# GpSimd's sums of the down weights: around the first reduction of the roots, or behind both

## The chip, the core and the metric

The kernel runs on one core of a Trainium2 chip. The metric is the time of one execution on the device in microseconds. TensorE is called PE here, VectorE DVE, ScalarE ACT, GpSimd POOL, and SyncE, which issues nearly all DMAs, SP.

## What is computed

A gated feed-forward layer with a condition and quantised activations, then an adapter. x is 2 x 2048 tokens of 512 values; the hidden width is 2048, the adapter's 128.

```python
scale = cond @ norm_w.T + 1.0
h = x * (scale[:, None, :] * rsqrt(mean(x * x, -1) + 1e-6))
val, gate = split(h @ up_w.T, 2)
h = val * gelu(gate)
hq = act_quant(h)              # per token: 127 / max|h|, rounded
wq = weight_quant(down_w)      # one scale for all: -1, 0 or 1
x = hq @ wq.T + x
# adapter, its weights made from cond: Wd + (cond @ Wdd.T + bdd) / 10, Wu alike
out = x + relu(x @ Wd_b.T + bd) @ Wu_b.T + bu
```

## The kernel before

The 4096 tokens are 8 blocks of 512 (0 to 7), handled as 4 super-blocks `s` of two blocks each. For each super-block a loop runs over 16 chunks `j` of the hidden width; iteration `n = 16 s + j` is called a quad. In a quad, PE computes the up projection of one chunk for both blocks with seven products instead of eight (Strassen's scheme in the form with sums of tiles). One product is six matmuls of 512 columns. Its order in quad n is: product 1 and 5 of n, product 3 of n-1, product 6 of n, product 4 of n-1, product 2 and 7 of n, then "side work". Product 4 of n-1 waits for `val2(n-1)` on DVE (L1886), and product 7 of n for `seed_c(n)` on DVE (L1878).

DVE's instructions of one quad stand in a fixed order: the rows of the down projection of the quad before (`first_rows`, L1993 and L1995), `quantise` (L1976), `assemble` (L2112 and L2113, in quads 28, 29, 43 and 45), `multiply2` of n-1 (L1917, waits for ACT's gelu of product 3), `seed_c` (L1878), `multiply1` (L1927), the two running maxima (L1941), then in quad 27 `x_scaled(4)` (four times L1839) and `spread_roots(5)` (L1822), in quad 28 `x_scaled(5)`, and then `val2(n)` (L1886). The tensors named `_ps` lie in PSUM, all others in SBUF.

Down projection: super-block 0 is done plainly as side work of quads 26 to 29 (L1426). Super-blocks 1 and 2 use seven products of half width, which need four sums of quarters of the quantised down weights `wq`. GpSimd makes these four sums once, in super-block 1: `down_sums(3)`, `(1)`, `(0)` and `(2)`, each one `tensor_tensor` of 128 x 2048 fp8 values (L941), into `w_sums`, which lies over buffers 2 and 3 of the ring `w_ring`. SP writes them to DRAM once (`put_sums_down`, L676 to L678), and later loads them back before they are used. The load of ring buffers 2 and 3 for adapter weights of quad 30 (`load_w(82)` and `(83)`, L615) waits until this put has landed.

The norm of super-block s+1 is prepared in super-block s. For blocks 4 and up, GpSimd does it in two steps by reductions over the partitions: `square_total(i)` (L919), and `root_rows(i)` (L926). `root_rows(4)` waits for DVE's `spread_roots(4)`, which is issued in quad 26; `x_scaled(4)` on DVE waits for it in quad 27; then comes `spread_roots(5)`, `root_rows(5)`, and `x_scaled(5)` in quad 28. GpSimd also reduces the running maxima once for each super-block (`all_h`, L908).

GpSimd's order in super-block 1 is: `all_h(0)`, `square_total(4)`, `square_total(5)`, `down_sums` 3, 1, 0, `root_rows(4)`, `down_sums(2)`, `root_rows(5)`. SP's order in quad 29 is: two puts of rows, `put_sums_down`, `load_e(31)`, `load_l(30)` (the split up weights; they wait for PE's product 6 and 4), two loads of rows; in quad 30: `load_w(80)` to `(83)`, two puts of rows.

Of the kernel before, what the change touches and what calls it, by code (L numbers as in the profile page):

```python
# [135 lines left out]
def next_groups(n):  # L136

    return next(groups_of_quad(q) for q in range(n, NQ) if q in DW_QUADS)
# [105 lines left out]
def build(nc, x, cond, norm_w, up_w, down_w, Wd, bd, Wu, bu, Wdd, bdd, Wdu, bdu, out):  # L244
    aux = aux_plan()
    aux_keys = list(aux)
    with ExitStack() as ctx:
# [287 lines left out]
        def _(sp):  # L535
# [140 lines left out]
            def put_sums_down():  # L676
                sp.wait_ge(s_wsum, 4)
                sp.dma_start(ws_dram, w_sums).then_inc(s_wsum_dma, 16)  # L678
# [90 lines left out]
            for n in range(NQ):  # L769
                s, j = divmod(n, NP)  # L770


                if n > NP + 1:
                    for g in groups_of_quad(n):
                        load_w(2 * g)
                        load_w(2 * g + 1)
                if s == 1 and j in DOWN_QUANTISE:
                    load_d(8 + DOWN_QUANTISE.index(j))
                if n:
                    for g in groups_of_quad(n - 1):  # L780
                        move(g)
                if s == 0:
                    if 1 <= j and j + 4 < NP:
                        load_u(j + 4)
                    if j:
                        put_l(j)
                    if n == 1 or n - 1 in DW_QUADS:
                        for g in next_groups(n):
                            load_w(2 * g)
                            load_w(2 * g + 1)  # L790
                    if j == 4:
                        put_sums()
                    if 3 <= j < 11:
                        load_d(j - 3)
                    if 1 <= j and j + 1 < NP:
                        put_e(j + 1)
                if s == 1 and Y_FIRST < j <= Y_FIRST + 4:
                    put_row(2 * (j - Y_FIRST - 1))
                    put_row(2 * (j - Y_FIRST - 1) + 1)
                if s == 1 and j == 13:  # L800
                    put_sums_down()
                if s > 1 and j == 10:
                    load_c11(s - 1)
                if s > 0 and j == 10 and s < NSB - 1:
                    load_base(s - 1)
                if s > 1 and j == 10:
                    load_sums_down(s - 1)
                if s > 1 and j == 11:
                    put_c11(s - 1)
                if s > 1 and j == 13:  # L810
                    load_c22(s - 1)
                    load_c21(s - 1)
                if s > 1 and j == 14:
                    put_c21(s - 1)
                if NP <= n + 2 < NQ:
                    load_e(n + 2)
                if NP <= n + 1 < NQ:
                    load_l(n + 1)
                if j in NEXT_X:
                    load_x(s + 1, NEXT_X[j])  # L820
                if s == 1 and Y_FIRST <= j < Y_FIRST + 4:
                    load_row(2 * (j - Y_FIRST))
                    load_row(2 * (j - Y_FIRST) + 1)
                if s > 1 and j == 11:
                    load_c12(s - 1)
                if s > 1 and j == 14:
                    put_second(s - 1)
                if n == max(ASSEMBLE) + 1:
                    load_ad(0)
                    load_ad(1)  # L830
                for at, i in MID_AT.items():
                    if n == at + 3:
                        put_ad(i)
                        if i == 0:
                            load_ad(2)
                if n == NQ - 2:
                    load_ad(3)
# [24 lines left out]
        @block.gpsimd  # L862
        def _(pool):
            pool.memset(ones[:, :], 1.0).then_inc(s_const, 1)
            pool.memset(ident[:, :], 1.0).then_inc(s_const, 1)
            pool.wait_ge(s_const, 2)
            pool.affine_select(out=ident[:, :], in_=ident[:, :], compare_op=ALU.is_equal, fill=0.0,
                               base=0, pattern=[[-1, P]], channel_multiplier=1).then_inc(s_const, 1)

            def a_block(j, half, which):  # L870
                return u_raw(j)[:, 2 * half:2 * half + 2, P * which:P * which + P]

            def weight_sums(j):

                pool.wait_ge(s_u[j % 4], 16 * (j // 4 + 1))
                if j == 2:

                    aux_ready(pool, "dw", 2)
                elif j == 4:
                    aux_ready(pool, "dw", 3)  # L880
                elif j == 0:

                    pool.wait_ge(s_seed_c, 1)
                elif j >= 3:
                    if j == 6:
                        pool.wait_ge(s_sums_lo, 2)
                    pool.wait_ge(s_ulo, part_count(j - 2, 3))
                s1, s2, s3, s4 = (s_sum(j, n, n + 1).rearrange("p (k m) -> p k m", k=2)
                                  for n in range(4))
                pool.tensor_tensor(s1, a_block(j, 0, 0), a_block(j, 1, 0), ALU.add)\  # L890
                    .then_inc(s_us, 1)
                pool.wait_ge(s_us, sum_count(j, 1))
                pool.tensor_tensor(s2, s1, a_block(j, 0, 1), ALU.subtract).then_inc(s_us, 1)
                pool.tensor_tensor(s3, a_block(j, 0, 1), a_block(j, 0, 0), ALU.subtract)\
                    .then_inc(s_us, 1)
                pool.wait_ge(s_us, sum_count(j, 2))
                pool.tensor_tensor(s4, a_block(j, 1, 1), s2, ALU.subtract).then_inc(s_us, 1)

            def all_h(s):

                if s:
                    pool.wait_ge(s_x1, 2 * KD * s)
                for t, s_max in ((1, s_max2), (0, s_max1)):
                    pool.wait_ge(s_max, NP * (s + 1))
                    if s == NSB - 1 and t == 0:

                        pool.wait_ge(s_step, 1)
                    pool.partition_all_reduce(yscale[:, TB * t:TB * t + TB],  # L908
                                              hmax[:, TB * t:TB * t + TB], P, AR.absmax)\
                        .then_inc(s_ma[t], 1)  # L910


            pool.wait_ge(s_rs, 2)
            for j in SUM_ORDER:
                weight_sums(j)
            def square_total(i):

                pool.wait_ge(s_sqp, (KD - 1) * (i - 1))
                pool.partition_all_reduce(res[:, 3, :], res[:, 2, :], P, AR.add)\  # L919
                    .then_inc(s_square_total, 1)  # L920

            def root_rows(i):

                pool.wait_ge(s_root_grid, i - 3)
                pool.wait_ge(s_xs, KD * i)
                pool.partition_all_reduce(res[:, 2, :], res[:, 3, :], P, AR.add)\  # L926
                    .then_inc(s_root_rows, 1)

            a11, a21, a12, a22 = (wq[:, HC * half:HC * half + HC, 2 * P * low:2 * P * low + 2 * P]
                                  for half in range(2) for low in range(2))  # L930

            def down_sums(m, left, right, op):

                if m == 3:
                    pool.wait_ge(s_wq, 8)
                    aux_ready(pool, "dw", AFTER_DOWN // 2 - 1)
                elif m == 1:
                    pool.wait_ge(s_wsum, 1)
                elif m == 0:
                    pool.wait_ge(s_wsum, 2)  # L940
                pool.tensor_tensor(w_sums[:, m, :, :], left, right, op, saturate=False)\  # L941
                    .then_inc(s_wsum, 1)

            for s in range(1, NSB):
                all_h(s - 1)
                if s + 1 < NSB:
                    for t in range(2):
                        square_total(2 * s + 2 + t)
                    if s == 1:
                        down_sums(3, a21, a22, ALU.add)  # L950
                        down_sums(1, w_sums[:, 3, :, :], a11, ALU.subtract)
                        down_sums(0, a12, w_sums[:, 1, :, :], ALU.subtract)
                    root_rows(2 * s + 2)
                    if s == 1:
                        down_sums(2, a11, a21, ALU.subtract)
                    root_rows(2 * s + 3)
            all_h(NSB - 1)

        @block.scalar
# [1413 lines left out]
```

## Time and profile before

| | |
|---|---|
| median of 3 runs | 840.19 us (839.9 to 841.25) |
| the profiled execution's own time | 839.96 us |
| its span, first to last instruction | 838.2 us |
| PE busy | 823.3 us, 98% |
| DVE busy | 661.7 us, 79% |
| ACT busy | 397.4 us, 47% |
| POOL busy | 119.9 us, 14% |
| DMA engines busy, slices 293 to 314, 314 to 335, 335 to 356 us | 6, 2 and 3 tenths |
| granted TensorE clock | 1.00 of full speed over the span |

Times of the profile are microseconds from the first instruction. A row of a timeline has the start, the duration, the engine, the line of the kernel, the operation, its output and inputs with their shapes, and in brackets how long the engine had been idle before and what ended that; "issue" stands for idle time that ended on nothing the profile shows. Neighbouring instructions of one kind are merged into one row ("x2"). A matmul's record is longer than the time to the next one's start, since they overlap.

### The profile page before, as it was taken

Reading aid. Unit: us, or ns where it says so; the run is one execution under the profiler, and the core shown is the slowest. Engines: PE = TensorE matmul, PEld = TensorE weight load, DVE = VectorE, ACT = ScalarE, POOL = GpSimd, SP = SyncE. Lnnn points to the kernel's source line nnn. Section 1 sums busy time; section 2 is a strip of 40 time slices with the busy share of each in tenths; the row PEclk is TensorE's granted clock in tenths of the full one; section 3 lists DMA queues with packets and bytes.
Section 4 is the critical chain, followed back from the end, with each engine's and each line's share of the span. In section 5 each row is a group of like instructions: output and inputs, shape, how many; then the busy total and the mean of one; then the engine's idle time right before and its main releaser. Section 6 shows DMA issues by size and latency. Waiting matters only on the chain.

```text
span 838.2 us, 11811 instructions
## 1 busy us (share of the span) xinstructions
PE 823.3 (98%) x3902; PEld 358.0 (43%) x3902; DVE 661.7 (79%) x964; ACT 397.4 (47%) x649; POOL 119.9 (14%) x91
## 2 busy tenths in 40 slices
PE   6999999999999999999999999999999999999998
PEld 4334444444444434444444444444444444444443
DVE  5997887989878889767777678988975666675986
ACT  5778887766455532227445543326433333324000
POOL 0363332302001053200101011100200000001000
PEclk9999999999999999999999999999999999999999
DMA  9879988666999862378798866337247444435232
GB/s 345 337 263 346 341 292 297 234 219 221 307 346 372 322 215 107 138 258 281 277 327 306 299 222 190 115 93 259 86 127 232 138 129 155 137 95 176 101 126 75
DMA packets 64859, 186.64 MB, mean 223 GB/s; under 512 B 7072, under 2 KB 8352, under 8 KB 64416
## 3 DMA queue, kind: packets, MB, share of 16 engines
q1 hardware_dynamic: 64512, 185.63, 63.9%
q8 instruction: 32, 0.52, 0.3%
q10 hardware_dynamic: 288, 0.26, 0.1%
q14 instruction: 27, 0.22, 0.1%
HBM read 154.41 MB, written 30.41 MB: 220 GB/s over the span
## 4 chain that ended last, share of the span: by engine, by line
PE 90%; DVE 2%; issue 2%; DVEq 0%
PE b_ps L1326 9%; PE b_ps L1328 9%; PE b_ps L1330 9%; PE a_ps L1326 6%; PE aux_ps L1381 6%; PE a_ps L1328 6%; PE a_ps L1330 6%; PE aux_ps L1439 6%; PE aux_ps L1526 3%; PE aux_ps L1517 3%; PE c_ps L1326 3%; PE e_ps L1328 3%; PE e_ps L1326 3%; PE e_ps L1330 3%; PE c_ps L1328 3%; PE c_ps L1330 3%
## 5 line engine op out<-in xcount | busy, mean ns | idle before, releaser
L1917 DVE SCALAR_TENSOR_TENSOR h_ring<-v_sb,unscale,gelu 128x512 f32<-128x512 f32 x63 | 55.1, 874 | 67.5 <-issue 35.4
L1326 PE MATMUL b_ps<-t_mov,u_l 128*128 128x512 f16 x252 | 95.5, 379 | 2.7 <-DVE c_ps L1878 2.7
L1330 PE MATMUL b_ps<-t_mov,u_l 128*128 128x512 f16 x252 | 95.5, 379 | 0.0
L1328 PE MATMUL b_ps<-t_mov,u_l 128*128 128x512 f16 x252 | 95.5, 379 | 0.0
L1941 DVE TENSOR_TENSOR hmax<-gelu,hmax 128x512 f32<-128x512 f32 x120 | 88.6, 740 | 7.8 <-ACT gelu L1090 2.9
L1060 ACT ACTIVATE b_ps<-a_ps 128x512 f32<-128x512 f32 x63 | 36.7, 582 | 99.1 <-PE a_ps L1330 99.1
L1094 ACT ACTIVATE gelu<-h_ring 128x512 f32<-128x512 f32 x64 | 40.3, 630 | 65.8 <-DVE h_ring L1917 65.8
L1976 DVE TENSOR_TENSOR h_ring<-h_ring,qscale 128x1024 f16<-128x1024 f32 x48 | 64.7, 1388 | 0.0
L1076 ACT ACTIVATE gelu<-a_ps,unscale 128x512 f32<-128x512 f32 x64 | 43.7, 682 | 43.4 <-DVE hmax L1941 41.1
L908 POOL PARTITION_ALL_REDUCE yscale<-hmax x8 | 17.9, 2267 | 321.4 <-DVE hmax L1941 320.7
L1090 ACT ACTIVATE gelu<-h_ring 128x512 f32<-128x512 f32 x64 | 40.2, 628 | 45.6 <-DVE h_ring L1927 45.3
L1927 DVE SCALAR_TENSOR_TENSOR h_ring<-b_ps,unscale,gelu 128x512 f32<-128x512 f32 x64 | 47.8, 747 | 16.1 <-PE b_ps L1330 15.8
L1084 ACT ACTIVATE gelu<-c_ps,unscale 128x512 f32<-128x512 f32 x64 | 43.9, 686 | 32.9 <-PE c_ps L1330 32.9
L1381 PE MATMUL aux_ps<-w_ring,cond_sb 128*32 128x512 f32 x480 | 58.3, 599 | 0.0
L1067 ACT ACTIVATE p_sb<-e_ps 128x512 f32<-128x512 f32 x63 | 37.5, 595 | 37.3 <-PE e_ps L1330 27.6
L1886 DVE TENSOR_TENSOR v_sb<-b_ps,p_sb 128x512 f32<-128x512 f32 x63 | 43.2, 686 | 11.3 <-PE b_ps L1330 11.1
L1326 PE MATMUL b_ps<-t_mov,u_e 128*128 128x512 f16 x126 | 47.8, 379 | 0.9 <-DVE t_mov L1870 0.9
L1326 PE MATMUL e_ps<-t_mov,u_e 128*128 128x512 f16 x126 | 47.8, 379 | 0.2 <-DVE u_e L1706 0.2
L1326 PE MATMUL a_ps<-t_mov,u_e 128*128 128x512 f16 x126 | 47.9, 381 | 0.0
L1328 PE MATMUL e_ps<-t_mov,u_e 128*128 128x512 f16 x126 | 47.8, 379 | 0.0
L1330 PE MATMUL e_ps<-t_mov,u_e 128*128 128x512 f16 x126 | 47.8, 379 | 0.0
L1326 PE MATMUL a_ps<-t_mov,u_l 128*128 128x512 f16 x126 | 47.8, 379 | 0.0
(253 smaller groups left out, 1690.3 us busy)
## 6 DMA issues: line engine op xcount, KB each, us to landing
w_ring<-in_Wdu SPq DMA_DIRECT2D x64, 512.0 KB, 6.2
w_ring<-in_Wdd SPq DMA_DIRECT2D x56, 512.0 KB, 7.2
u_l<-ul_dram SPq DMA_DIRECT2D x48, 512.0 KB, 4.7
u_e<-ue_dram SPq DMA_DIRECT2D x48, 384.0 KB, 3.2
h_ring<-in_up_w SPq DMA_DIRECT2D x16, 512.0 KB, 6.5
x_sb<-in_x SPq DMA_DIRECT2D x8, 1024.0 KB, 8.2
res<-in_down_w SPq DMA_DIRECT2D x16, 512.0 KB, 7.4
ul_dram<-u_l SPq DMA_DIRECT2D x15, 512.0 KB, 5.7
```

The costliest lines, as they stand in the source:

```text
L1076: act.activation(gelu1[:, :], a_ps[n % 2][:, :], ACT.Gelu, scale=unscale[:, s // 2, j:j + 1]).then_inc(s_g1, 1)
L1084: act.activation(gelu2[:, :], c_ps[:, :], ACT.Gelu, scale=unscale[:, s // 2, j:j + 1]).then_inc(s_g2, 1)
L1326: pe.matmul(ps[:, :], weight(n, p, 0, k), hi, start=fresh and k == 0, stop=False, skip_group_check=True)
L1328: pe.matmul(ps[:, :], weight(n, p, 0, k), lo, start=False, stop=False, skip_group_check=True)
L1330: mm = pe.matmul(ps[:, :], weight(n, p, 1, k), hi, start=False, stop=k == 1, skip_group_check=True)
L1381: mm = pe.matmul(ps[32 * q:32 * q + 32, :], cond_sb[:, :], w_tile(n)[:, 512 * (q % 2):512 * (q % 2) + 512], start=True, stop=True)
L1439: mm = pe.matmul(ps[:, :], w, q_slot(d, at + c)[:, TB * t:TB * t + TB], start=fresh and c == 0, stop=c == HC - 1, skip_group_check=True)
L1886: dve.tensor_tensor(v_sb[:, :], b_ps[n % 2][:, :], p5_sb[:, :], ALU.add)\
L1917: dve.scalar_tensor_tensor(out=h_slot(n)[:, TB:TS], in0=val[:, :], scalar=unscale[:, s // 2, j:j + 1], in1=gelu2[:, :], op0=ALU.mult, op1= ...
L1927: dve.scalar_tensor_tensor(out=h_slot(n)[:, 0:TB], in0=b_ps[n % 2][:, :], scalar=unscale[:, s // 2, j:j + 1], in1=gelu1[:, :], op0=ALU.mul ...
L1941: dve.tensor_tensor(total, absolute, total, ALU.max).then_inc(done, 1)
L1976: dve.tensor_tensor(q_slot(s, c), h_slot(NP * s + c), qscale[:, :], ALU.mult)\
```

## The change

In GpSimd's program both `root_rows` of the super-block now come ahead of all four `down_sums`; before, three sums stood ahead of the first and one between the two. In super-block 2, which has no sums, the order is as it was. In SP's program `put_sums_down` moves within quad 29 from ahead of `load_e(31)` to behind the two loads of rows.

```diff
                 if s == 1 and Y_FIRST < j <= Y_FIRST + 4:
                     put_row(2 * (j - Y_FIRST - 1))
                     put_row(2 * (j - Y_FIRST - 1) + 1)
-                if s == 1 and j == 13:
-                    put_sums_down()
                 if s > 1 and j == 10:
                     load_c11(s - 1)
...
                 if s == 1 and Y_FIRST <= j < Y_FIRST + 4:
                     load_row(2 * (j - Y_FIRST))
                     load_row(2 * (j - Y_FIRST) + 1)
+                if s == 1 and j == 13:
+                    put_sums_down()
...
                 if s + 1 < NSB:
                     for t in range(2):
                         square_total(2 * s + 2 + t)
+                    for t in range(2):
+                        root_rows(2 * s + 2 + t)
                     if s == 1:
                         down_sums(3, a21, a22, ALU.add)
                         down_sums(1, w_sums[:, 3, :, :], a11, ALU.subtract)
                         down_sums(0, a12, w_sums[:, 1, :, :], ALU.subtract)
-                    root_rows(2 * s + 2)
-                    if s == 1:
                         down_sums(2, a11, a21, ALU.subtract)
-                    root_rows(2 * s + 3)
```

## Rows read from the trace of the kernel before

**Rows 1.** Waits of PE, 200 to 400 us: us in total, times, longest.

```profile
PE b_ps L1326 <- DVE c_ps L1878: 1.7, 2, 1.3
```

**Rows 2.** Timeline of GpSimd, 300 to 345 us: start, us, engine, line, idle before.

```profile
305.04 3.82 POOL L941 TENSOR_TENSOR w_ring<-wq 128x2048 fp8e4<-128x2048 fp8e4 x1 [9.62 <-issue]
308.94 4.17 POOL L941 TENSOR_TENSOR w_ring<-w_ring,wq 128x2048 fp8e4<-128x2048 fp8e4 x1
313.18 4.16 POOL L941 TENSOR_TENSOR w_ring<-wq,w_ring 128x2048 fp8e4<-128x2048 fp8e4 x1
323.12 3.25 POOL L926 PARTITION_ALL_REDUCE res<-res  x1 [5.79 <-issue]
334.29 3.82 POOL L941 TENSOR_TENSOR w_ring<-wq 128x2048 fp8e4<-128x2048 fp8e4 x1 [7.91 <-issue]
```

**Rows 3.** Timeline of DVE beside GpSimd's operations, 305 to 338 us.

```profile
305.78 3.63 DVE L1917 SCALAR_TENSOR_TENSOR h_ring<-v_sb,unscale,gelu 128x512 f32<-128x512 f32 x1 [1.89 <-issue]
...
310.59 3.05 DVE L1941 TENSOR_TENSOR hmax<-gelu,hmax 128x512 f32<-128x512 f32 x1
...
313.57 4.31 DVE L1941 TENSOR_TENSOR hmax<-gelu,hmax 128x512 f32<-128x512 f32 x1
...
323.76 2.15 DVE L1917 SCALAR_TENSOR_TENSOR h_ring<-v_sb,unscale,gelu 128x512 f32<-128x512 f32 x1
...
335.80 0.69 DVE L1995 TENSOR_TENSOR res<-aux_ps,res 128x512 f32<-128x512 f32 x1
336.40 2.25 DVE L2112 TENSOR_TENSOR l_wd<-l_wd,w_ring 128x512 f32<-128x512 f32 x1
```

**Rows 4.** Timelines of DVE and PE: the two product 7 that waited.

```profile
309.33 0.69 DVE L1878 TENSOR_TENSOR c_ps<-b_ps,p_sb 128x512 f32<-128x512 f32 x1
...
310.17 0.38 PE L1326 MATMUL b_ps<-t_mov,u_l 128*128 128x512 f16 x1 [1.32 <-DVE c_ps L1878]
...
326.66 0.38 PE L1326 MATMUL b_ps<-t_mov,u_l 128*128 128x512 f16 x1 [0.36 <-DVE c_ps L1878]
```

**Rows 5.** Timelines of DVE and PE in iterations 28 and 29.

```profile
342.21 1.47 DVE L1941 TENSOR_TENSOR hmax<-gelu,hmax 128x512 f32<-128x512 f32 x2
...
347.29 2.74 DVE L1839 SCALAR_TENSOR_TENSOR x_sb<-res,cs_x,x_sb 128x512 f32<-128x512 f32 x4 [3.61 <-POOL res L926]
...
349.94 0.68 DVE L1886 TENSOR_TENSOR v_sb<-b_ps,p_sb 128x512 f32<-128x512 f32 x1
...
355.70 0.75 DVE L1917 SCALAR_TENSOR_TENSOR h_ring<-v_sb,unscale,gelu 128x512 f32<-128x512 f32 x1 [1.09 <-ACT gelu L1084]
356.37 0.69 DVE L1878 TENSOR_TENSOR c_ps<-b_ps,p_sb 128x512 f32<-128x512 f32 x1
...
342.63 0.38 PE L1326 MATMUL b_ps<-t_mov,u_l 128*128 128x512 f16 x1
...
358.60 0.38 PE L1326 MATMUL b_ps<-t_mov,u_l 128*128 128x512 f16 x1
```

**Rows 6.** Timelines of DVE (both super-blocks) and GpSimd around spread_roots.

```profile
331.12 0.68 DVE L1822 TENSOR_TENSOR res<-ident,rs 128x512 f32<-128x512 f32 x1
...
514.52 0.69 DVE L1822 TENSOR_TENSOR res<-ident,rs 128x512 f32<-128x512 f32 x1
...
515.31 3.23 POOL L926 PARTITION_ALL_REDUCE res<-res  x1 [23.15 <-DVE res L1822]
```

**Rows 7.** Timelines of SP's queue and PE: put, weight loads, use.

```profile
353.70 0.43 SPq L678 DMA_DIRECT2D ws_dram<-w_ring  x1
...
358.88 3.05 SPq L615 DMA_DIRECT2D w_ring<-in_Wdu  x4
...
375.96 1.92 PE L1381 MATMUL aux_ps<-w_ring,cond_sb 128*32 128x512 f32 x16
```

**Rows 8.** Timeline of PE near the start: single and merged.

```profile
17.88 0.63 PE L1364 MATMUL a_ps<-t_mov,u_e 128*128 128x512 f16 x1
...
18.31 1.06 PE L1368 MATMUL a_ps<-t_mov,u_e 128*128 128x512 f16 x2
```
## The prediction

> **What bounds the kernel now.** I read the page's busy shares first: PE is busy 98% of the span, so a microsecond counts only if PE stands still for it or stops standing still. The waits of PE between 200 and 400 us come next: one kind is left there, product 7's first matmul waiting for DVE's `seed_c` (L1878), twice [rows 1]. The timeline of GpSimd shows why to look at DVE: the three sums of `down_sums` lie at 305.04 to 317.34, the fourth at 334.29, and the first `root_rows` reduction at 323.12 [rows 2]. Beside them DVE's operations with two SBUF inputs are stretched. L1917 takes 3.63 us and ends 0.55 us behind the first sum; the two L1941 take 3.05 and 4.31 us and end 0.53 and 0.54 us behind the second and the third; L1917 takes 2.15 us beside a reduction; L2112 takes 2.25 us beside the fourth sum [rows 3]. L1995, with one input in PSUM, takes its usual 0.69 us beside that same sum [rows 3]. So while GpSimd runs a sum, a DVE operation with two SBUF inputs waits until it ends. The two engines take turns too: the third sum began at 313.18, was let in between two L1941 that DVE had back to back, and the second of these waited for it. One turn costs 313.18 - 308.94 = 4.24 us; DVE, whose own operation would have taken 0.67 of it, loses 3.57.
>
> **What the change removes.** Both stalls of PE come from this. The first sum holds L1917 of iteration 26, so `seed_c` is late and PE stands 1.32 us before product 7; `root_rows(4)` holds L1917 of iteration 27 and costs 0.36 us [rows 4]. A matmul is recorded 0.38 us long and the next starts 0.22 us behind it, so each idle time hides 0.16 us more: 1.48 + 0.52 = 2.00 us. With the sums gone from there, `seed_c` of iteration 26 isn't held, DVE ends its list earlier, and `root_rows(4)` needs no change of GpSimd's code ahead of it (the reduction before it is of the same kind), so it runs earlier by what the three sums held DVE (2.9, 2.3 and 3.6 us over the usual times of these operations), near 314, beside no L1917. Both stalls go: -2.0 us. What is late next there is L1917 itself, which waits for ScalarE's gelu, and then has 1.4 us to spare before product 7 (in iteration 29 `seed_c` ends at 357.06, PE could start 0.15 behind, and product 7 starts at 358.60 [rows 5]). The wait of `x_scaled(5)` for `root_rows(5)`, 3.61 us [rows 5], goes too, but PE never felt it: worth nothing by itself.
>
> **Where the sums land.** `root_rows(5)` starts when `spread_roots(5)` ends; in the next super-block, where no sum is in the way, the reduction of `root_rows(6)` starts 0.1 us behind L1822 [rows 6]. DVE comes to `spread_roots(5)` (L1822) at 331.12 before [rows 6]. Its list then hangs on product 7 of iteration 27, which moves from 326.66 to 324.66, and by the pattern of iteration 28, where L1941 starts 0.42 us before product 7 (342.21 against 342.63 [rows 5]), x_scaled(4) and the spread follow by 328.96. The reduction runs 3.25 us: 329.1 to 332.3. Now GpSimd changes from the code of the reduction to that of the element-wise sum. The profile shows this as idle time on "issue": 9.62 and 7.91 us in this direction, 5.79 us in the other [rows 2]. By the page's slices the DMA engines were 6 tenths busy around the longest and 2 tenths around the other; where the changed kernel's falls they are 2 to 3 tenths busy, so 9.62 is the less likely of the two, and the code of the first sum may come sooner than either. I bound it by 5.8 and 7.9 us, with 9.6 as a tail, and take the middle, 6.9 us: **the first sum starts at 339.2** (338.1 to 340.2, tail 341.9). [...]
>
> **What it costs there.** In iteration 28, all 2.0 us earlier than before, DVE has ahead of it: two L1941 at 340.2 (1.47 us), four L1839 of `x_scaled(5)` (2.65 us for the four), `val2` L1886 (in PSUM), four operations of y rows (in PSUM), L2112, L2113, L1917, `seed_c` [rows 5]. The first six have two SBUF inputs. One passes per sum: the first sum ends at 343.0 and lets one L1941 end at 343.6; the second ends at 347.3, L1941 at 347.8; the third at 351.5, L1839 at 352.0; the fourth at 355.7, L1839 at 356.3. The two L1839 left take until 357.5, where `val2` starts. From the start of `val2` to the end of L2113 are 4.67 us (349.94 to 354.61, where the idle time ahead of L1917 begins), then L1917 0.67 and `seed_c` 0.69, and PE 0.15 behind (`seed_c` ended at 310.02, product 7 began at 310.17): 6.2 us [rows 4, 5]. Product 7 of iteration 29 can start at 363.7. Unheld it would start at 358.60 - 2.00 = 356.6 [rows 5]. Loss: 7.1 us, seen as two waits: product 4 of iteration 28 needs `val2` (358.2 + 0.15, against 354.0, twelve matmuls of 0.216 us ahead of product 7: some 4.4 us), and product 7 `seed_c` (some 2.7 us). The same from the other side: the first L1941 is held 2.7 us (340.9 to 343.6) and three operations 3.57 us each, 13.4 in all; DVE's slack in this stretch is 3.61 us of idle before L1839, 1.09 before L1917 and 1.4 before product 7, 6.1 in all: 7.3. **Sum: -2.0 + 7.1 = +5.1 us.** By the bounds of the code change it is +4.0 (start 338.1) to +6.1 (start 340.2).
>
> **The put.** In the diff `put_sums_down` moves behind load_e(31), load_l(30) and the two loads of rows in SP's iteration 29, so from 353.70 to just ahead of 358.88, 5.1 us later; load_w(82) and (83) wait for it and stand ahead of put_row(6), (7). The four weight loads were issued by 361.9 and first used at 375.96 [rows 7]: 14 us of cover, of which 5 go, and PE is 5 us later itself. GpSimd ends the sums at some 355.7, before SP comes to that wait. Nothing for the put. With its cover gone it would cost a microsecond for each late. What load_e(31) and load_l(30) gain by standing ahead is nothing either: they wait for PE's own products. After the sums GpSimd has nothing until the super-block's last maximum, three quads on, so a code change back is hidden.
>
> **Rivals.**
> - *The sums start later than L1941.* If the code takes 9.6 us again, both L1941 and one L1839 are through; three sums hold three L1839, `val2` is at 355.1, and the fourth runs beside the rows in PSUM and holds L2112 only to 359.3. Product 7 starts at 361.5: loss 4.9, net +3.0: 843.2 us. For it: both rows of this direction; against: the DMA load around the 9.6.
> - *The clock.* PE stands over 4 us in one piece. After the standstill at the start of the kernel two matmuls of 512 columns take 1.06 us together and one of them 0.63 [rows 8]: they start 0.43 apart, against 0.22 elsewhere: the 1.2 GHz level, though the granted clock reads 1.00. If that comes back here, product 4 and 2 (12 matmuls, 2.6 us more) hide under the second wait, product 7's six and up to twelve of the next rows don't: +1.3 to +3.9, 846.6 to 849.2, likeliest 847.9. Against: no stall above 1.5 us lies inside the kernel to judge by. [...]
> - *Faster.* The turns go to DVE: if GpSimd waits whenever DVE has the next operation of two SBUF inputs ready, the sums just stretch, nobody waits for them, and only the 2.0 us gain stays: 838.2 us. It decides where the sums hold no more than two of the nine such operations up to `seed_c` (7.2 us, against 6.1 of slack and 2.0 won). Against it: the third sum got in between two L1941.
> - *Nothing.* The first sum starts behind 344, past x_scaled: holds of 1.2, 3.6 and 3.6 us on L2112, L2113 and L1917, less 6.1, are 2.3 us against 2.0 won: 840.5.
>
> **How the numbers follow.** Forecast: 840.19 + 5.1 = 845.3 us (the profiled run was 839.96, with a span of 838.2; the median is 0.2 above it, so 845.1 for a run like it). Chances: the forecast's case (start 337 to 341.5) 0.60, later start 0.15, clock 0.10, nothing 0.05, faster 0.10. Range 841.6 to 848.6: it takes in the forecast's bounds (844.2 to 846.3), the later start, and most of the clock case, and leaves the last two out. Slower by over 0.2% (1.7 us, about what can be told from no change here) 0.85, within 0.05, faster 0.10.
>
> **What would show it.** In the profile after: no wait of PE for c_ps L1878 near 309 and 325; `root_rows(4)` near 313.7 and (5) near 329; the first sum near 339 and the four 4.2 us apart; L1941 and L1839 of 3 to 4 us beside them; two waits of PE of about 4.4 and 2.7 us near 354 and 361, on L1886 and L1878; SP's ws_dram issue behind the row loads with no long wait. Wrong if L1839 keeps its 0.75 us beside a sum, if the four sums are far more than 4.2 us apart, or if PE waits for w_ring near 377.

## The result, and the profile after

The changed kernel takes 845.36 us (median of 6 runs, 844.8 to 847.48) against 840.26 us of the kernel before (6 runs, 839.41 to 842.54): a ratio of 1.0064, with a 95% interval of 1.0052 to 1.0076. It is slower by 5.4 us by the ratio. The profiled execution took 846.51 us. Line numbers from 956 on are one lower than before (L1886 is L1885, L1878 is L1877, L1941 is L1940, L1839 is L1838, L1917 is L1916).

The page of the kernel after: span, busy shares of PE, and the granted clock in 40 slices.

```profile
span 844.8 us, 11807 instructions
...
PE 826.8 (98%) x3902; PEld 358.5 (42%) x3902; DVE 663.0 (78%) x964; ACT 397.6 (47%) x649; POOL 121.8 (14%) x91
...
PEclk9999999999999999989999999999999999999999
```

PE's busy share is as it was, but one slice shows a lower clock, and the share of 98% hides a stall of over 4 us. The waits of PE from 200 to 400 us show it. The two stalls of [rows 1] are gone, and another stands in their place: product 4 of quad 28 waits for `val2(28)`.

```profile
PE b_ps L1325 <- DVE v_sb L1885: 4.2, 1, 4.2
```

GpSimd's timeline (start, duration, engine, line, operation, idle before). Both reductions stand ahead of the sums; `root_rows(4)`, at 323.12 in [rows 2], is at 315.03, and the idle time between the last reduction and the first sum is 6.91 us, less than the 7.91 and 9.62 of [rows 2]. In GpSimd's queue two instructions `MODIFY_POOL_CONFIG`, issued for the sums' line L941, stand at 333.6, where the second reduction ends. In the kernel before such a pair stands ahead of each of the four idle times: for L941 at 295.4 and 326.4 (9.62 and 7.91 us), for L926 at 317.5 and 338.3 (5.79 and 5.90 us). In neither kernel does one stand between two sums, nor in the changed one ahead of `root_rows(4)` at 315.03, which follows another reduction. This is what "code change" means here; what GpSimd does in the idle time is not in the trace. The four sums start 3.9 to 4.2 us apart.

```profile
315.03 3.23 POOL L926 PARTITION_ALL_REDUCE res<-res  x1 [18.14 <-DVE res L1821]
330.42 3.23 POOL L926 PARTITION_ALL_REDUCE res<-res  x1 [12.16 <-DVE res L1821]
340.56 3.82 POOL L941 TENSOR_TENSOR w_ring<-wq 128x2048 fp8e4<-128x2048 fp8e4 x1 [6.91 <-issue]
344.46 4.16 POOL L941 TENSOR_TENSOR w_ring<-w_ring,wq 128x2048 fp8e4<-128x2048 fp8e4 x1
348.70 4.16 POOL L941 TENSOR_TENSOR w_ring<-wq,w_ring 128x2048 fp8e4<-128x2048 fp8e4 x1
352.82 4.27 POOL L941 TENSOR_TENSOR w_ring<-wq 128x2048 fp8e4<-128x2048 fp8e4 x1
```

DVE's timeline beside them. Each of the first four operations with two SBUF inputs waits for one sum, just as in [rows 3], and ends 0.55 us behind it: both running maxima (L1940) and two of the four L1838 of `x_scaled(5)`. The last two take their usual time, then come `val2(28)` (L1885) and, 5.2 us later, `seed_c(29)` (L1877).

```profile
341.58 3.35 DVE L1940 TENSOR_TENSOR hmax<-gelu,hmax 128x512 f32<-128x512 f32 x1
...
344.86 4.31 DVE L1940 TENSOR_TENSOR hmax<-gelu,hmax 128x512 f32<-128x512 f32 x1
349.09 4.32 DVE L1838 SCALAR_TENSOR_TENSOR x_sb<-res,cs_x,x_sb 128x512 f32<-128x512 f32 x1
...
353.33 4.31 DVE L1838 SCALAR_TENSOR_TENSOR x_sb<-res,cs_x,x_sb 128x512 f32<-128x512 f32 x1
...
358.89 0.68 DVE L1885 TENSOR_TENSOR v_sb<-b_ps,p_sb 128x512 f32<-128x512 f32 x1
...
364.13 0.69 DVE L1877 TENSOR_TENSOR c_ps<-b_ps,p_sb 128x512 f32<-128x512 f32 x1
```

PE's timeline: product 4 starts at 359.71, behind `val2(28)`, which ended at 359.57. From there to the second matmul of product 7 the records last some 0.6 us and the starts lie 0.43 us apart (360.09, 360.51, 360.94), not 0.22. Product 7 starts at 364.97, where [rows 5] had 358.60. It still goes by `seed_c(29)`, which ended at 364.82, 0.15 us before; no idle time stands between, since slow matmuls had filled the wait but for the last 0.2 us.

```profile
359.71 0.58 PE L1325 MATMUL b_ps<-t_mov,u_l 128*128 128x512 f16 x1 [4.16 <-DVE v_sb L1885]
360.09 0.63 PE L1327 MATMUL b_ps<-t_mov,u_l 128*128 128x512 f16 x1
...
364.36 0.63 PE L1329 MATMUL a_ps<-t_mov,u_l 128*128 128x512 f16 x1
364.97 0.58 PE L1325 MATMUL b_ps<-t_mov,u_l 128*128 128x512 f16 x1
...
366.47 7.07 PE L1425 MATMUL aux_ps<-h_ring,wq 128*128 128x512 f16 x32
```

The stretch from 350 to 372 us and the part of it from 360 to 364 us (length, busy times, granted clock, DMA share, GB/s): the granted clock is 0.84 over the whole and 0.50 over the part. It was 1.00 before.

```profile
350.00:372.00 22.00, 17.84 (x70) 7.14 (x69) 18.65 (x19) 3.70 (x6) 7.09 (x2) 0.84 0.44 149
360.00:364.00 4.00, 4.00 (x11) 1.39 (x10) 3.90 (x7) 0.83 (x2) 0.00 (x0) 0.50 0.42 145
```

The put was issued at 364.71, where [rows 7] had 353.70. The four weight loads behind it took 9.70 us to issue, because two of them wait for the put, and they are first used at 382.54. PE did not wait for them. (PE's one wait for `w_ring` in this trace, 0.18 us, lies at 268.22, far ahead of the change.)

```profile
364.71 0.43 SPq L678 DMA_DIRECT2D ws_dram<-w_ring  x1
365.24 9.70 SPq L615 DMA_DIRECT2D w_ring<-in_Wdu  x4
...
382.54 1.92 PE L1380 MATMUL aux_ps<-w_ring,cond_sb 128*32 128x512 f32 x16
```

The rows of y of quads 27 to 29 (the L1425 group of PE) measure the loss without the rest of the run. Undisturbed they are 15.97 us apart; here those of quads 28 and 29 start at 343.30 and 366.47, 23.17 apart: **7.2 us are lost in quad 29.** The execution as a whole is 1.4 us late by quad 26 from something else: in quad 22 PE and its weight loader waited for a late load of adapter weights. That is a matter of this one execution (`e5_after_again` is 0.4 us late there), and it is why the span grew by 6.6 us while the medians are 5.1 apart.

### The profile page after: what moved, and what is told of

Its sections match the earlier page's. It is cut to its first block, busy times and chain, and to the rows that moved or that the text cites. A ratio compares the mean times of both kernels' runs of the same rounds, so it can differ in the third digit from the quotient of the medians.

```text
span 844.8 us, 11807 instructions
## 1 busy us (share of the span) xinstructions
PE 826.8 (98%) x3902; PEld 358.5 (42%) x3902; DVE 663.0 (78%) x964; ACT 397.6 (47%) x649; POOL 121.8 (14%) x91
## 4 chain that ended last, share of the span: by engine, by line
PE 89%; DVE 2%; DMA 1%; issue 1%; SPq 0%; DVEq 0%
PE b_ps L1325 9%; PE b_ps L1329 9%; PE b_ps L1327 9%; PE a_ps L1325 6%; PE aux_ps L1380 6%; PE a_ps L1329 6%; PE a_ps L1327 6%; PE aux_ps L1438 6%; PE aux_ps L1525 3%; PE aux_ps L1516 3%; PE c_ps L1325 3%; PE c_ps L1327 3%; PE c_ps L1329 3%; PE e_ps L1325 3%; PE e_ps L1329 3%; PE e_ps L1327 3%
## 5 line engine op out<-in xcount | busy, mean ns | idle before, releaser
L1916 DVE SCALAR_TENSOR_TENSOR h_ring<-v_sb,unscale,gelu 128x512 f32<-128x512 f32 x63 | 50.9, 808 | 73.4 <-ACT gelu L1083 37.9
L1940 DVE TENSOR_TENSOR hmax<-gelu,hmax 128x512 f32<-128x512 f32 x120 | 89.0, 743 | 7.9 <-ACT gelu L1089 3.0
L908 POOL PARTITION_ALL_REDUCE yscale<-hmax x8 | 17.8, 2260 | 318.1 <-DVE hmax L1940 317.5
L1885 DVE TENSOR_TENSOR v_sb<-b_ps,p_sb 128x512 f32<-128x512 f32 x63 | 43.2, 686 | 11.2 <-PE b_ps L1329 11.0
L1325 PE MATMUL a_ps<-t_mov,u_l 128*128 128x512 f16 x126 | 48.3, 383 | 0.0
L1327 PE MATMUL a_ps<-t_mov,u_l 128*128 128x512 f16 x126 | 48.3, 383 | 0.0
L1329 PE MATMUL a_ps<-t_mov,u_l 128*128 128x512 f16 x126 | 48.3, 383 | 0.0
L1325 PE MATMUL e_ps<-t_mov,u_e 128*128 128x512 f16 x126 | 47.8, 379 | 0.5 <-DVE u_e L1705 0.5
```

The source lines that it names most:

```text
L1325: pe.matmul(ps[:, :], weight(n, p, 0, k), hi, start=fresh and k == 0, stop=False, skip_group_check=True)
L1327: pe.matmul(ps[:, :], weight(n, p, 0, k), lo, start=False, stop=False, skip_group_check=True)
L1329: mm = pe.matmul(ps[:, :], weight(n, p, 1, k), hi, start=False, stop=k == 1, skip_group_check=True)
L1885: dve.tensor_tensor(v_sb[:, :], b_ps[n % 2][:, :], p5_sb[:, :], ALU.add)\
L1916: dve.scalar_tensor_tensor(out=h_slot(n)[:, TB:TS], in0=val[:, :], scalar=unscale[:, s // 2, j:j + 1], in1=gelu2[:, :], op0=ALU.mult, op1= ...
L1940: dve.tensor_tensor(total, absolute, total, ALU.max).then_inc(done, 1)
```

## The experiments

The theory: GpSimd and DVE take turns by whole instructions, so every sum holds one DVE operation with two SBUF inputs, and the sums now stand where six such operations precede `val2(28)` and nine precede `seed_c(29)`. The rivals: the later put makes the loss; the reductions or the code change make it; GpSimd's busy time counts, whatever its pieces. Ratios are against runs of the kernel before on the same chip, each with its 95% interval.

### The two halves of the change

Only GpSimd's order (`e1_order_only`):

```diff
                     put_row(2 * (j - Y_FIRST - 1) + 1)
+                if s == 1 and j == 13:
+                    put_sums_down()
...
                     load_row(2 * (j - Y_FIRST) + 1)
-                if s == 1 and j == 13:
-                    put_sums_down()
```

> The changed kernel with put_sums_down in its old place, so only GpSimd's order is changed. Theory (the holds of DVE by the sums make all of the loss, the put makes none): 845.3 us, between 844.5 and 846; SP reaches the put behind the end of the sums and does not wait; the wait of 0.2 us of PE for w_ring may go. Rival (the later put makes a part of the loss, since the weight loads queue behind it): 840.5 to 844.

Measured: 845.91 us, ratio 1.0069 (1.0056 to 1.0082). Only the put, `e2_put_only`, is the same edit the other way round on the kernel before.

> The kernel before with only the put moved behind the two loads of rows; GpSimd's order is the old one. Theory: 840.2 us, no change that can be measured (839.5 to 841), both old stalls of PE before product 7 stay. Rival (the put costs): 842 or more.

Measured: 839.33 us, ratio 0.9999 (0.9990 to 1.0008), with both old stalls in place. So the whole loss is GpSimd's order; the put neither costs nor gains anything beyond the 0.8 us of that interval. It isn't unseen, though: in its new place it took 8.6 us to land (9.4 in the changed kernel), beside the loads issued just around it, where before it took 4.2. Two of the weight loads wait for it, but PE does not.

PE's timeline of `e1_order_only` holds one thing more. The clock stays up for the first two matmuls after the wait and falls from the third (359.44) on; it recovers at 362.85, before product 7, which therefore shows a wait of its own for `seed_c(29)`.

```profile
359.01 0.38 PE L1325 MATMUL b_ps<-t_mov,u_l 128*128 128x512 f16 x1 [3.93 <-DVE v_sb L1885]
...
359.87 0.63 PE L1325 MATMUL b_ps<-t_mov,u_l 128*128 128x512 f16 x1
...
364.27 0.38 PE L1325 MATMUL b_ps<-t_mov,u_l 128*128 128x512 f16 x1 [0.82 <-DVE c_ps L1877]
```

### The sums taken away (e3_small_sums) and two of them (e6_two_sums)

```diff
-                pool.tensor_tensor(w_sums[:, m, :, :], left, right, op, saturate=False)\
+                cut = (slice(0, 1), slice(0, 32)) if m in (0, 1, 2, 3) else (slice(0, HC), slice(0, 2 * P))
+                pool.tensor_tensor(w_sums[:, m, cut[0], cut[1]], left[:, cut[0], cut[1]],
+                                   right[:, cut[0], cut[1]], op, saturate=False)\
                     .then_inc(s_wsum, 1)
```

In `e6_two_sums` the condition is `m in (0, 2)`. The sums that run first, `down_sums(3)` and `(1)`, are then whole. Both kernels leave most of the cut sums unmade, and both put `wq` to DRAM in place of `w_sums`.

> The changed kernel with each of the four sums cut to 32 values of each partition, and the put taken from wq instead of w_sums, so the products of the down projection that use the sums are not those of the reference. All semaphores, waits, the code change of GpSimd and the size of the put are kept. Theory: no hold of DVE is left, the gain of the two old stalls stays alone: 840.2 - 2.0 = 838.2 us, no wait of PE for L1877 or L1885 between 300 and 370 us. Rival (the loss comes from the later reductions, the code change or the put): 843 to 845.

Measured: 838.54 us, ratio 0.9984 (0.9975 to 0.9993). GpSimd and DVE in it: the first sum still comes 7.09 us behind the reduction, the first small sum lasts 0.23 us, and the maxima and the four L1840 (`x_scaled(5)`) take their usual times. PE waits for nothing there.

```profile
339.88 0.23 POOL L942 TENSOR_TENSOR w_ring<-wq 128x32 fp8e4<-128x32 fp8e4 x1 [7.09 <-issue]
...
340.72 1.47 DVE L1942 TENSOR_TENSOR hmax<-gelu,hmax 128x512 f32<-128x512 f32 x2
342.11 2.73 DVE L1840 SCALAR_TENSOR_TENSOR x_sb<-res,cs_x,x_sb 128x512 f32<-128x512 f32 x4
```

> The changed kernel with the first two of the four sums at full size and the other two cut to 32 values a partition; the put comes from wq, so the products that use the sums are not those of the reference. Theory (one DVE operation is held for each full sum, first 2.7 then 3.57 us, against 6.1 us of slack): 6.3 - 6.1 = 0.2 us of wait, so 840.2 - 2.0 + 0.2 = 838.4 us, no wait of PE for L1885 near 355. Rival (each sum costs its share of the 7.1 us, two of them 3.5): 841.7 us.

Measured: 839.10 us, ratio 0.9983 (0.9973 to 0.9992). The first two sums hold both maxima (7.55 us instead of 1.47), and the loss ends there: `x_scaled(5)` is free, DVE works without a gap into L1918 (`multiply2`), and PE has no wait in this stretch. `seed_c(29)` ends at 356.39, 0.33 us before product 7 starts at 356.72, so the slack is nearly used up.

```profile
340.32 7.55 DVE L1942 TENSOR_TENSOR hmax<-gelu,hmax 128x512 f32<-128x512 f32 x2
347.80 2.73 DVE L1840 SCALAR_TENSOR_TENSOR x_sb<-res,cs_x,x_sb 128x512 f32<-128x512 f32 x4
...
355.04 0.74 DVE L1918 SCALAR_TENSOR_TENSOR h_ring<-v_sb,unscale,gelu 128x512 f32<-128x512 f32 x1
```

6.1 us of delay cost nothing, all four sums cost 7: what counts is the delay above DVE's slack, not a share for each sum. The rival that wanted 3.5 us for two sums falls, and the code change and the moved reductions, present here and in `e3_small_sums`, are cleared as well.

### The sums in pieces (e4_split_sums, e10_two_pieces, e11_split_again)

```diff
-                pool.tensor_tensor(w_sums[:, m, :, :], left, right, op, saturate=False)\
-                    .then_inc(s_wsum, 1)
+                for c in range(0, HC, HC // 8):
+                    part = slice(c, c + HC // 8)
+                    pool.tensor_tensor(w_sums[:, m, part, :], left[:, part, :],
+                                       right[:, part, :], op, saturate=False)\
+                        .then_inc(s_wsum, 1)
```

The three waits on `s_wsum` count eight times as far (twice in `e10_two_pieces`, where 8 is 2).

> The changed kernel with each sum issued as eight instructions of 256 values a partition instead of one of 2048; the same work. Theory (the two engines take turns by whole instructions): a DVE operation with two SBUF inputs waits for one piece at most, about 0.5 us; up to nine such operations lose 4.5 us at most, less than the slack of 6.1: no wait of PE, 838.2 us. Rival (GpSimd's busy time beside DVE counts, whatever its pieces): the sums take 16 to 18 us as before, DVE is held as long, 845 us.

Measured: 839.00 us, ratio 0.9985 (0.9976 to 0.9993). The same work now takes GpSimd 24 us instead of 16, and DVE loses 0.4 us on the maxima (1.86 instead of 1.47) and 1.5 on `x_scaled(5)` (4.26 instead of 2.73). The rival that counts GpSimd's busy time falls: there is more of it, and PE doesn't wait. The put now waits for the last piece and is issued at 364.09; the last weight load behind it is issued at 369.8, for a use that starts at 374.39, so its cover is down to 4.6 us.

```profile
339.67 7.51 POOL L943 TENSOR_TENSOR w_ring<-wq 128x256 fp8e4<-128x256 fp8e4 x8 [6.95 <-issue]
...
359.24 4.82 POOL L943 TENSOR_TENSOR w_ring<-wq 128x256 fp8e4<-128x256 fp8e4 x8
...
340.64 1.86 DVE L1943 TENSOR_TENSOR hmax<-gelu,hmax 128x512 f32<-128x512 f32 x2
342.42 4.26 DVE L1841 SCALAR_TENSOR_TENSOR x_sb<-res,cs_x,x_sb 128x512 f32<-128x512 f32 x4
```

> The changed kernel with each sum in eight pieces, once more, for a narrower interval against the kernel before and beside the other two: 838.9 us, a ratio of 0.9985.

Measured: 838.41 us, ratio 0.9988 (0.9979 to 0.9997). With its two intervals just below 1, this version beats both kernels, if by only 0.12 to 0.15% of the time of the kernel before.

> The changed kernel with each sum issued as two instructions of 1024 values a partition. Theory of turns: a held DVE operation waits for one piece, 1.9 us and a little, and loses 1.7 us; two L1940 and four L1838 lose 9.4 us before val2(28), less 6.1 us of slack: 3.3 us of the 7.1 are left: 840.2 - 2.0 + 3.3 = 841.5 us. Rival (GpSimd's busy time beside DVE counts): 845.5 us. Rival (any split cures it): 838.8 us.

Measured: 843.25 us, ratio 1.0042 (1.0029 to 1.0055), 3.5 us slower: between the two rivals, as the theory wants, but more than the 1.3 us forecast. Both rivals fall. DVE shows where the time goes. The pieces and their turns were longer than half a sum (4.41 to 4.75 us a pair), the maxima lost 3.1 us and `x_scaled(5)` 7.0, and a later piece held one assemble operation (L2114) for 0.5: 10.6 us in all instead of 9.4.

```profile
339.78 4.54 DVE L1943 TENSOR_TENSOR hmax<-gelu,hmax 128x512 f32<-128x512 f32 x2
344.24 9.73 DVE L1841 SCALAR_TENSOR_TENSOR x_sb<-res,cs_x,x_sb 128x512 f32<-128x512 f32 x4
...
354.72 0.38 PE L1328 MATMUL b_ps<-t_mov,u_l 128*128 128x512 f16 x1 [0.97 <-DVE v_sb L1888]
...
360.50 0.38 PE L1328 MATMUL b_ps<-t_mov,u_l 128*128 128x512 f16 x1 [3.03 <-DVE c_ps L1880]
```

PE's two waits, 0.97 and 3.03 us, are some 4.3 us with the overlap, 1.0 more than forecast. With the gain that makes +2.3, and the profiled execution, at 842.09 us the fastest of five, lies 2.6 above the median before. The other four took 842.78 to 843.90, and the two longest of them are the only ones with a granted clock of 0.998 in place of 1.00. So a fall of the clock, absent in the profile, may be a part of the 3.5 us; no trace of those two runs shows it.

### The old order with pieces (e9_split_old_order)

The same split on the kernel before.

> The kernel before (old order and old place of the put) with each sum issued as eight instructions of 256 values a partition. Theory: DVE is no longer held by a sum, but the reductions now stand behind sums that give way to DVE: three sums of 6 to 7 us and two code changes put root_rows(4) near 330 and root_rows(5) near 352, where x_scaled(4) and x_scaled(5) wait for them at 326 and 342; val2(28) and seed_c(29) come some 3 and 8 us late: about 846 us, between 843 and 847. Rival (splitting alone is enough, whatever the order): 838.5 to 839.

Measured: 845.54 us, ratio 1.0070 (1.0056 to 1.0084). The reductions now stand behind sums that yield at every turn, and DVE waits for them, 4.28 and 10.53 us, as the timelines of GpSimd, DVE and PE show.

```profile
326.58 3.25 POOL L926 PARTITION_ALL_REDUCE res<-res  x1 [5.82 <-issue]
...
349.69 3.25 POOL L926 PARTITION_ALL_REDUCE res<-res  x1 [6.15 <-issue]
...
329.86 2.74 DVE L1842 SCALAR_TENSOR_TENSOR x_sb<-res,cs_x,x_sb 128x512 f32<-128x512 f32 x4 [4.28 <-POOL res L926]
...
352.97 2.74 DVE L1842 SCALAR_TENSOR_TENSOR x_sb<-res,cs_x,x_sb 128x512 f32<-128x512 f32 x4 [10.53 <-POOL res L926]
...
356.46 0.58 PE L1329 MATMUL b_ps<-t_mov,u_l 128*128 128x512 f16 x1 [2.40 <-DVE v_sb L1889]
```

PE waits 2.40 us for `val2(28)` and then 0.97 for `seed_c(29)`, and the rows of quads 28 and 29 are 21.20 us apart: 5.2 lost, where the expectation had some 8. The time fell inside its range, but the profiled execution was the fastest of five (843.50 us), and 2 us of the median are not in its trace.

So the order of the changed kernel is right for short instructions and wrong for long ones. Pieces alone don't help, and the order alone doesn't: here the two are worth something only together.

### The place of the sums (e7_sums_behind_x_scaled)

```diff
                     pool.wait_ge(s_wq, 8)
+                    pool.wait_ge(s_xs, KD * 6)
```

> The changed kernel with one more wait of GpSimd: the first sum waits until x_scaled(5) has finished on DVE. Theory, with the code change done before that wait ends: the sums start some 3 us behind the maxima, hold the two assemble operations and L1916 of quad 29 (0.6, 3.6 and 3.6 us) and not the four of x_scaled; product 7 waits some 1.4 us instead of 7: 839.6 us. If the code change begins only after the wait, the sums start near 352, hold L1916 for under 2 us, PE waits for nothing there, but the put lands after 378 and the weight loads behind it make PE wait for w_ring in quad 30, 1 to 4 us: 839 to 842 us. Rival (place makes no difference, the sums cost 7 us wherever they lie behind the reductions): 845 us.

Measured: 846.87 us, ratio 1.0083 (1.0070 to 1.0096). My forecast of 839.6 was wrong. The code change was over (the first sum starts at 346.15, 0.2 us behind the last L1839), but I had counted slack that lies in front of the held operations. DVE had nothing to do for much of the first two sums but operations with PSUM and a wait of 2.03 us for PE's rows (L1993). The other two sums and the end of the second one then fell on L2112, L2113 and L1917, behind which there is 1.9 us of slack before L1917 (the idle time there in `e3_small_sums`, 1.91) and 1.4 before product 7.

```profile
346.15 3.83 POOL L942 TENSOR_TENSOR w_ring<-wq 128x2048 fp8e4<-128x2048 fp8e4 x1 [12.19 <-issue]
...
350.71 0.70 DVE L1993 TENSOR_TENSOR aux_ps<-aux_ps,yscale 128x512 f32<-128x512 f32 x1 [2.03 <-PE aux_ps L1426]
...
352.06 2.38 DVE L2112 TENSOR_TENSOR l_wd<-l_wd,w_ring 128x512 f32<-128x512 f32 x1
354.47 4.20 DVE L2113 SCALAR_TENSOR_TENSOR l_wd<-l_wd,w_ring 128x512 f32<-128x512 f32 x1
358.59 4.30 DVE L1917 SCALAR_TENSOR_TENSOR h_ring<-v_sb,unscale,gelu 128x512 f32<-128x512 f32 x1
...
363.65 0.59 PE L1326 MATMUL b_ps<-t_mov,u_l 128*128 128x512 f16 x1 [5.20 <-DVE c_ps L1878]
...
366.16 8.50 PE L1426 MATMUL aux_ps<-h_ring,wq 128*128 128x512 f16 x32
```

The holds are 1.7, 3.5 and 3.6 us, 8.8 together; less 3.3 they give 5.5, and PE waits 5.2 + 0.16. The place of that wait matters too: it lies before product 7, and no later wait follows for slow matmuls to hide in. The clock falls after it, product 7's matmuls start 0.43 apart and take 2.51 us instead of 1.30, and the L1426 group takes 8.50 us instead of 7.07. That is 1.2 + 1.4 = 2.6 us of clock, in the open. In all 8.0 us are lost in quad 29; less a gain of 1.0 to 2.0 that makes 6 to 7, and the ratio gives 7.0. (The profiled execution, 849.27 us, was the slowest of five; a late load of weights in quad 22 made it over 1 us later than most by quad 26.)

### Is the slow spell hidden? (e5_after_again, e8_assemble_early)

The slow spell is the stretch behind PE's wait in which matmuls start 0.43 us apart (granted clock 0.50).

> The changed kernel once more, beside the three variants of it that run on the same chip. Both theories: 845.4 us (844.5 to 846).

Measured: 845.65 us, ratio 1.0070 (1.0058 to 1.0082). Here the slow spell ended at 361.68, and product 7 waited 1.06 us for `seed_c(29)` (timeline of PE). From the rows of quad 28 to those of quad 29 are 22.98 us: 7.0 us lost, as with the longer spell (7.2).

```profile
361.68 0.39 PE L1327 MATMUL a_ps<-t_mov,u_l 128*128 128x512 f16 x1
...
364.00 0.38 PE L1325 MATMUL b_ps<-t_mov,u_l 128*128 128x512 f16 x1 [1.06 <-DVE c_ps L1877]
```

The variant of the changed kernel:

```diff
-ASSEMBLE = {28: 0, 29: 1, 43: 2, 45: 3}
+ASSEMBLE = {27: 0, 28: 1, 43: 2, 45: 3}
```

> The changed kernel with the two assemble steps in quads 27 and 28 instead of 28 and 29, which takes 1.4 us of DVE work out of the way of seed_c(29). Theory with the clock (after its wait of 4 us PE starts matmuls 0.43 us apart, and product 2 ends about when seed_c does): product 7 is then bound by product 2 in executions in which the clock stays down so long, so only 0.2 to 1 us of the 1.4 come back: 844.4 to 845.2 us; in the profile the matmuls of product 4 and 2 start 0.43 apart and no wait of PE for L1877 is left in quad 29. Theory without the clock (the wait for seed_c alone sets product 7): 844.0 us.

Measured: 844.89 us, ratio 1.0060 (1.0048 to 1.0072). The intervals of this and of `e5_after_again` overlap, so the times alone don't decide between the expectations; the profile does for its own execution. `seed_c(29)` ends at 362.45, yet product 7 starts only at 363.63, straight behind the last slow matmul of product 2, with no idle time.

```profile
361.76 0.69 DVE L1877 TENSOR_TENSOR c_ps<-b_ps,p_sb 128x512 f32<-128x512 f32 x1
...
363.31 0.48 PE L1329 MATMUL a_ps<-t_mov,u_l 128*128 128x512 f16 x1
363.63 0.38 PE L1325 MATMUL b_ps<-t_mov,u_l 128*128 128x512 f16 x1
```

So in this execution the slow matmuls set the start, and of the 1.4 us taken off DVE's path nearly nothing came back: 22.89 us between the rows, against 22.98. The slow matmuls took 1.0 of it (363.63, where `seed_c` would have allowed 362.60), and 0.2 went because the sums started 0.2 us later within the quad. With the wait for `seed_c` in place they cost next to nothing; without it they take its place. The six timed runs point the same way, though they are few: the three with a granted clock of 0.998 took 844.20 to 844.65 us, the three with 0.996 took 845.13 to 846.85. The runs of the changed kernel show no such order.

## Why the prediction was right

- **What the change removes.** The two stalls are gone in every profile of the new order, and 15.97 us from the rows of quad 26 to those of quad 27 (311.36 to 327.33) show it. As a term of the sum it was set at -2.0 us. Measured where PE has no wait in the stretch, it is 1.0 to 1.4 us: ratios 0.9984, 0.9985, 0.9983 and 0.9988. Three of these four intervals reach 2.0 us or just past it, the fourth ends at 1.8. In the four profiles PE has no wait before product 7 of quad 26, and the rows of quads 26 to 29 are 15.97 or 15.98 us apart each time, so the stretch itself gives the whole 2.0. Up to a microsecond of it isn't seen in the medians; where it goes isn't settled. These profiles differ from the one before by up to 0.5 us ahead of the stretch and up to 1.0 behind it, too much to find it there.
- **Where the sums land.** The first sum was put at 339.2, by a code change of 6.9 us. It came at 340.56, in an execution 1.4 us late, and at 339.60 in `e5_after_again`, 0.4 us late. The idle times were 6.91 and 6.93 us, and 6.7 to 7.5 in all the other runs in which the first sum follows both reductions and waits for nothing else. The prediction weighed its cases by the DMA load, but read that load from slices of 21 us: "2 tenths" around the 7.91 us. In the window of that change itself (326.40 to 334.30) the DMA share was 0.42; in that of the changed kernel it was 0.20.
- **What it costs there.** Four holds, on exactly the two maxima and the first two operations of `x_scaled(5)`. Forecast loss 7.1 us; measured 7.2 and 7.0. First wait of PE forecast at 4.4 us, measured 4.16 + 0.16. This is the term that carries the result.
- **The second wait** was forecast at 2.7 us. It shrank to 0.2 us in the first profile (where the list of waits has none), is 0.82 us in `e1_order_only` and 1.06 in `e5_after_again`. The difference is the clock. I gave it a chance of 0.10 as a case of its own, with 1.3 to 3.9 us on top. It happened in every profile of the changed kernel, and the granted clock was 0.996 to 0.998 in all six timed runs. For the fall of the clock that chance was far too low, though the price that went with it did not come. The "1.2 GHz level" of that rival is an estimate, 512 columns in 0.43 us (1.19 a nanosecond); no profile gives a frequency, only the spacing and the granted clock. In `e10_two_pieces` a wait of 3.03 us left the clock up. The first part of that rival's working was right: product 4 and 2 hide under the second wait. The second was wrong: the clock was back up at product 7 or by its second matmul, so nothing or 0.2 us went on top.
- **The sum** rests on the right mechanism, but its close hit, 845.36 for 845.3, is in part luck. By the medians the gain was 0.6 to 1 us smaller than its term and the loss as forecast, so the sum should have come out at some 6 us. It measured 5.4 and 5.9 us, with intervals of about 1 us on either side that hold both 6 and the forecast 5.1, so these runs don't tell the two apart.
- **The put** costs nothing, as forecast, though its cover was thinner than thought: the last of the weight loads behind it was issued at 374.9 for a use that starts at 382.54, 7.6 us instead of the 14 of before, with 5 expected to go.
- **Rivals.** The later start, the faster case and the case of nothing did not occur; the turns went as forecast, one held operation for each whole sum. The price of *nothing* (sums behind `x_scaled`, 840.5 us) was mis-sized: it subtracted all 6.1 us of slack from holds that come behind most of it. With the sums there, `e7_sums_behind_x_scaled` took 846.87.

## What to carry to other kernels

In these runs an element-wise GpSimd instruction beside a busy VectorE acts as a turn: each one holds at most one DVE operation with two SBUF inputs, until it ends. Cutting long ones into pieces took away nearly all of the hold, but the pieces together take longer, so anything that stands behind them on GpSimd comes later (`e9_split_old_order`). When placing them, count the slack only from the first operation held. And look at what follows a stall of PE: in `e7_sums_behind_x_scaled` 8.8 us of holds cost more than 13.3 did in the changed kernel, in part because the clock fell (2.6 us) and no second wait followed to hide the slow matmuls.

## What the runs showed of the hardware

- The change of GpSimd's code from a reduction to an element-wise operation took longer the busier the DMA engines were: 6.7 to 7.5 us at DMA shares of 0.10 to 0.26 within its own window, 7.9 and 8.4 at 0.40 to 0.42, 9.4 to 9.7 at 0.57 (three executions, around 300 us). That the DMA load is the cause is not shown; no run changed it alone. The other direction took 5.8 to 6.2. The change runs ahead while GpSimd waits for a semaphore: in `e7_sums_behind_x_scaled` `MODIFY_POOL_CONFIG` stands at 333.9, and the first sum came 0.2 us behind its releaser at 346.0.
- PE's matmuls started 0.43 us apart instead of 0.22, at a granted clock of 0.50, behind waits of 2.40 us (`e9_split_old_order`), 3.9 to 4.4 us (the changed kernel, `e1_order_only`, `e8_assemble_early`) and 5.20 us (`e7_sums_behind_x_scaled`), and kept their 0.22 behind 0.97 and 3.03 us (`e10_two_pieces`). So the length of a wait alone doesn't tell whether the clock falls. The slow spells lasted from 2.9 to 5.6 us where product 4 and 2 followed. At the kernel's start the same spacing of 0.43 us lasts from 17.03 to 20.87 with a granted clock of 1.00, so the granted clock doesn't show every slow stretch.
- A reduction holds DVE for less than it lasts: L1917 at 323.76, beside the reduction from 323.12 to 326.37, ended at 325.91 [rows 2, 3]. The sums held to their end and 0.55 us beyond. L1917 ended 0.46 us before the record of the reduction did; no run shows why.
- Two SBUF inputs are not the whole of what is held: beside the pieces of `e9_split_old_order`, 128x8 operations of DVE with one SBUF input (`TENSOR_SCALAR`, L1800 to L1803, from 310.67) took 0.56 us each, where the kernel before has 0.15 to 0.17 (L1797 to L1800).
- One GpSimd sum of 2048 fp8 values a partition takes 3.82 us alone, and 256 values take 0.63 to 0.64: cutting it eightfold costs GpSimd 1.0 to 3.7 us a sum, with DVE's turns, and DVE 1.9 us in all on the maxima and `x_scaled(5)` (`e4_split_sums`).
